# Routing weights on the down sums: router and experts of a fused attention and FFN kernel put into one block

## What is computed

```
x = x + ao @ wo
h = _rmsnorm(x, ln2_w)
logits = h @ router_w
probs = jax.nn.softmax(logits, axis=-1)
topv, topi = jax.lax.top_k(probs, TOPK)
topv = topv / jnp.sum(topv, axis=-1, keepdims=True)
weights = jnp.sum(jax.nn.one_hot(topi, E, dtype=h.dtype) * topv[..., None], axis=-2)
gate = jnp.einsum('bsd,edm->bsem', h, w_gate)
up = jnp.einsum('bsd,edm->bsem', h, w_up)
act = jax.nn.silu(gate) * up * weights[..., None]
moe = jnp.einsum('bsem,emd->bsd', act, w_down)
return x + moe
```

## Time and profile before

| | |
|---|---|
| median of three runs | 717.56 us |
| traced span of the profiled execution | 711.4 us |
| what lies around the span, by the median | 6.2 us |
| PE, DVE, ACT, POOL busy in the span | 602.2, 587.9, 454.6, 227.9 us |
| routing and logits, first logit matmul to the last weight | 548.5 to 556.4 us |
| weight columns spread by TensorE | 557.2 to 568.0 us |
| expert slabs, first gate matmul to last down matmul | 568.3 to 704.7 us |

### The profile page before, as it was taken

How to read it: one execution, slowest core, us unless ns; L and a number is a source line. 1 busy time by engine, 2 the same in 40 slices (tenths; PEclk the granted TensorE clock), 3 DMA queues, 4 the chain that set the end, 5 groups by cost and what they waited for, 6 DMA issues and landing times. The chain is left out here.

```text
span 711.4 us, 13311 instructions
## 1 busy us (share of the span) xinstructions
PE 602.2 (85%) x3580; PEld 492.3 (69%) x3580; DVE 587.9 (83%) x1282; ACT 454.6 (64%) x1094; POOL 227.9 (32%) x435
## 2 busy tenths in 40 slices
PE   2979889988999999899999336899997689797996
PEld 2757778767887778778787325666666577575885
DVE  4768899878898788998889747899983599979995
ACT  3657777766777677767777125888883356344563
POOL 1553334323333333333335354722132321414000
PEclk9989999999999999999999868999998699998999
DMA  8020000000000000000000002000000220200000
GB/s 255 17 54 2 2 29 3 1 1 0 0 30 0 1 0 0 0 0 1 1 1 1 1 4 82 1 1 0 0 0 1 78 77 2 77 1 0 0 0 29
DMA packets 15342, 13.48 MB, mean 19 GB/s; under 512 B 1984, under 2 KB 14656, under 8 KB 15296
## 3 DMA queue, kind: packets, MB, share of 16 engines
q1 hardware_dynamic: 15072, 12.94, 6.2%
q10 hardware_dynamic: 224, 0.03, 0.0%
HBM read 12.44 MB, written 0.52 MB: 18 GB/s over the span
## 5 line engine op out<-in xcount | busy, mean ns | idle before, releaser
L516 ACT ACTIVATE p_raw<-bank,bias 128x512 f32<-128x512 f32 x128 | 87.7, 688 | 43.1 <-DVE bias L587 39.4
L582 DVE TENSOR_REDUCE neg_max<-bank 128x1 f32<-128x512 f32 x128 | 86.9, 679 | 5.9 <-issue 4.0
L657 POOL TENSOR_SCALAR p_norm<-p_raw,rinv 128x512 f32<-128x512 f32 x128 | 87.0, 692 | 0.1
L606 DVE TENSOR_TENSOR pT_lo<-bank,pT_hi 128x512 fp32r<-128x512 f32 x128 | 82.4, 685 | 3.9 <-issue 2.3
L534 ACT ACTIVATE pT_hi<-bank 128x512 fp32r<-128x512 f32 x128 | 69.7, 599 | 24.9 <-PE bank L439 23.4
L1472 ACT ACTIVATE act_hi<-act_f 128x512 fp32r<-128x512 f32 x56 | 35.4, 632 | 58.9 <-DVE act_f L1515 58.8
L439 PE MATMUL bank<-ident,p_norm 128*128 128x128 f32 x512 | 66.8, 273 | 0.4 <-DVE pT_lo L606 0.4
L439 PEld LDWEIGHTS bank<-ident,p_norm 128*128 128x128 f32 x512 | 59.8, 141 | 9.3 <-issue 1.2
L451 PE MATMUL bank<-pT_hi,vals 128*128 128x256 f32 x256 | 64.9, 286 | 1.5 <-DVE o_lo L598 1.5
L451 PE MATMUL bank<-pT_lo,vals 128*128 128x256 f32 x256 | 64.0, 283 | 0.0
L426 PE MATMUL bank<-keys,q_hi 128*128 128x512 f32 x128 | 54.7, 427 | 3.0 <-ACT p_raw L516 2.8
(11 more groups left out here) (272 smaller groups left out, 1731.3 us busy)
## 6 DMA issues: line engine op xcount, KB each, us to landing
ctx_raw<-in_ctx SPq DMA_DIRECT2D x4, 512.0 KB, 4.7
wkv_raw<-in_L_xattn_Wkv SPq DMA_DIRECT2D x2, 1024.0 KB, 11.1
gu_raw<-in_L_ffn_w_gate SPq DMA_DIRECT2D x4, 448.0 KB, 3.6
gu_raw<-in_L_ffn_w_up SPq DMA_DIRECT2D x4, 448.0 KB, 4.3
dn_raw<-in_L_ffn_w_down SPq DMA_DIRECT2D x4, 448.0 KB, 5.1
wout_raw<-in_L_xattn_Wout SPq DMA_DIRECT2D x2, 512.0 KB, 14.8
x<-in_x SPq DMA_DIRECT2D x1, 512.0 KB, 6.8
wq_raw<-in_L_xattn_Wq SPq DMA_DIRECT2D x1, 512.0 KB, 10.2
```

The costliest lines, as they stand in the source:

```text
L516: act.activation(p_raw[:, h % 2, t, :], s_bank[t][:, :], ACT.Exp, bias=bias[:, h % H, t:t + 1], scale=X_SCALE, accum_out=row_sum[:, h % H, ...
L582: dve.tensor_reduce(neg_max[:, h % H, t:t + 1], s_bank[t][:, :], AX_X, ALU.max, negate=True).then_inc(max_s, 1)
L606: dve.tensor_tensor(pT_lo[:, h % 2, 2 * half:2 * half + 2, :], t_bank[half][:, :].rearrange("p (j n) -> p j n", j=2), f(pT_hi[:, h % 2, 2 ...
L657: pool.tensor_scalar(p_norm[:, h % 2, t, :], p_raw[:, h % 2, t, :], rinv[:, h % H, t:t + 1], 1.0, ALU.mult, ALU.mult).then_inc(p_norm_s, 1)
```

## The change

`route` and `experts` become one function, `route_and_experts`, with one block, and its loops are unrolled.

- The weights multiply the down sums. Slabs are taken in the order 0, 1, 2, 4, 5, 6, 3. The three slabs of one expert add up in their own bank `y_bank`; then VectorE's `weigh(i)` makes y_w = y_bank x wide, and GpSimd's `add(i)` adds it onto `acc` in SBUF. There are 16 such sums. Only the mixed slab, now the last of each seven, keeps up_w, and alone goes to `d_bank`.
- act_f of the other slabs is made from `u_bank` in PSUM and gate, in one operation. `u_bank` and `g_bank` are two deep instead of three.
- `wide` and `wide_mix` come by DMA: weights (128 tokens x 8) are transposed into 8 rows, copied to SBUF and to DRAM (`weight_rows`), and read back to all partitions by sixteen transfers on SP, two per expert. The fetches of the pairs 1 to 3 stand behind them on SP.
- The router's softmax and top two run on VectorE behind the first act_f; gate and up of the first slabs stand ahead of them on TensorE. h2T_lo is made by VectorE instead of GpSimd.
- The residual x1 + x2 is made by GpSimd (`x_sum`, behind the split of pair 1) and added by VectorE at the very end.

Its core; the routing arithmetic itself is unchanged:

```diff
+        g_bank, u_bank, y_bank, d_bank = ([bank(f"{n}_bank{i}") for i in range(2)] for n in "guyd")
...
+        SLAB = [*range(MIXED), *range(MIXED + 1, SLABS), MIXED]
+        U, UNITS_ALL = CH * SLABS, PAIRS * CH * SLABS
+        YS = PAIRS * CH * 2
...
         def _(sp):
-            with sp.Fori(1, PAIRS) as g:
+            sp.wait_ge(wT_s, CH)
+            sp.dma_start(rows, wT[:, :]).then_inc(rows_out, 16)
+            sp.wait_ge(rows_out, 16)
+            for g in range(PAIRS):
+                for i in range(2):
+                    e = 2 * g + i
+                    sp.dma_start(wide[:, e, :], rows[e, :].partition_broadcast(P)).then_inc(wide_in[g], 16)
+                    part = slice(0, SPLIT) if i == 0 else slice(SPLIT, P)
+                    sp.dma_start(wide_mix[part, g, :], rows[e, :].partition_broadcast(part.stop - part.start)).then_inc(wide_in[g], 16)
+            for g in range(1, PAIRS):
                 sp.wait_ge(k.split_s, g)
                 fetch_pair(sp, k, dram, g)
             for c in range(CH):
...
+                if n >= 2:
+                    pe.wait_ge(silu_s, n - 1)
+                    pe.wait_ge(mul_s, n - 1)
...
+            def down(n):
+                g, c, s = where(n)
+                pe.wait_ge(a_lo_s, n + 1)
+                i = expert_sum(n)
+                if i is None:
+                    to, first, done = d_bank[c], g == 0, g == PAIRS - 1
+                else:
+                    to, first, done = y_bank[i % 2], n % SLABS % MIXED == 0, n == last_slab(i)
+                    if first and i >= 2:
+                        pe.wait_ge(y_out_s, i - 1)
...
+            def weights_first():
+
+                pe.wait_ge(weights_s, 1)
+                for t in range(TT):
+                    last = pe.transpose(w_bank[t // 4][0:E, (t % 4) * P:(t % 4 + 1) * P], weights[:, t, :], k.ident[:, :])
+                    if t % 4 == 3:
+                        last.then_inc(wT_ps, 1)
...
+            for n in range(UNITS_ALL + 2):
+                if n < UNITS_ALL:
+                    gate_up(n)
+                if n == 2:
+                    weights_first()
+                if n >= 2:
+                    down(n - 2)
+                if n == UNITS_ALL - SLABS + 4:
+                    tokens_first(0)
...
+            def weights_first():
+
+                for c in range(CH):
+                    act.wait_ge(wT_ps, c + 1)
+                    act.activation(wT[:, c * BANK:(c + 1) * BANK], w_bank[c][0:E, :], ACT.Copy).then_inc(wT_s, 1)
...
+            for n in range(UNITS_ALL + 1):
+                if n >= 1:
+                    head(n - 1)
+                if n < UNITS_ALL:
+                    silu(n)
+                if n == 2:
+                    weights_first()
...
             split_pair(pool, k, 1, 1)
...
+            pool.tensor_tensor(x_sum[:, :, :], k.x1[:, :, :], x2[:, :, :], ALU.add).then_inc(x_sum_s, 1)
+
+            def add(i):
+
+                c = i // 2 % CH
+                pool.wait_ge(y_out_s, i + 1)
+                if i // 2 < CH and i % 2 == 0:
+                    pool.tensor_scalar(acc[:, c, :], y_w[:, i % 2, :], 1.0, 1.0, ALU.mult, ALU.mult).then_inc(added_s, 1)
+                else:
+                    pool.wait_ge(added_s, i)
+                    pool.tensor_tensor(acc[:, c, :], acc[:, c, :], y_w[:, i % 2, :], ALU.add).then_inc(added_s, 1)
+
+            for i in range(YS):
+                add(i)
+                if i % 4 == 3 and i // 4 + 2 < PAIRS:
+                    g = i // 4 + 2
+                    split_pair(pool, k, g, g % 2, (down_ps, (g - 1) * U))
...
+            def product(n):
+                g, c, s = where(n)
+                dve.wait_ge(gu_ps, n + 1)
+                if n >= 2:
+                    dve.wait_ge(a_lo_s, n - 1)
+                up = u_bank[n % 2][:, :]
+                if s == MIXED:
+                    dve.wait_ge(wide_in[g], 4 * 16)
+                    dve.tensor_tensor(up_w[:, :], up, wide_mix[:, g, c * BANK:(c + 1) * BANK], ALU.mult).then_inc(weighed_s, 1)
+                    dve.wait_ge(weighed_s, n // SLABS + 1)
+                    up = up_w[:, :]
+                dve.wait_ge(silu_s, n + 1)
+                dve.tensor_tensor(act_f[:, n % 2, :], up, gate[:, n % 2, :], ALU.mult).then_inc(mul_s, 1)
+
+            def tail(n):
+                dve.wait_ge(a_hi_s, n + 1)
+                dve.tensor_tensor(act_lo[:, n % 2, :], act_f[:, n % 2, :], f(act_hi[:, n % 2, :]), ALU.subtract).then_inc(a_lo_s, 1)
+
+            def weigh(i):
+
+                g, c, _ = where(last_slab(i))
+                dve.wait_ge(down_ps, last_slab(i) + 1)
+                dve.wait_ge(wide_in[g], 4 * 16)
+                if i >= 2:
+                    dve.wait_ge(added_s, i - 1)
+                dve.tensor_tensor(y_w[:, i % 2, :], y_bank[i % 2][:, :], wide[:, 2 * g + i % 2, c * BANK:(c + 1) * BANK], ALU.mult)\
+                    .then_inc(y_out_s, 1)
+
+            def summed(c):
+                dve.wait_ge(added_s, YS - (CH - 1 - c) * 2)
+                dve.wait_ge(down_ps, UNITS_ALL - (CH - 1 - c) * SLABS)
+                dve.tensor_tensor(sumT[:, c * BANK:(c + 1) * BANK], d_bank[c][:, :], acc[:, c, :], ALU.add).then_inc(sumT_s[c], 1)
+
+            def finished(c):
+                dve.wait_ge(out_ps, c + 1)
+                dve.wait_ge(x_sum_s, 1)
+                dve.tensor_tensor(res[:, 4 * c:4 * c + 4, :], by_tile(d_bank[c]), x_sum[:, 4 * c:4 * c + 4, :], ALU.add).then_inc(res_s[c], 1)
+
+            shifted_logits()
+            for n in range(UNITS_ALL + 3):
+                if 1 <= n <= UNITS_ALL:
+                    tail(n - 1)
+                if n < UNITS_ALL:
+                    product(n)
+                if n == 0:
+                    routing_weights()
+                if n >= 3 and (n - 3) % SLABS in (MIXED - 1, 2 * MIXED - 1):
+                    weigh(expert_sum(n - 3))
+                if n == UNITS_ALL - SLABS + 3:
+                    summed(0)
+                if n == UNITS_ALL - SLABS + 5:
+                    finished(0)
+            summed(1)
+            finished(1)
```

More of the change, by code:

```diff
@@ L1377, in _, with last_slab, half @@
+        def last_slab(i):
+            return i // 2 * SLABS + (i % 2 + 1) * MIXED - 1
+        def half(i):
+            return range(4 * i, 4 * i + 4)
         @block.sync
         def _(sp):
-            with sp.Fori(1, PAIRS) as g:
+            sp.wait_ge(wT_s, CH)
[8 more added lines that the diff above has]
+            for g in range(1, PAIRS):
@@ new lines, in _ @@
+            for i in range(2):
+                t = slice(4 * i, 4 * i + 4)
+                pool.wait_ge(sq_s, i + 1)
+                pool.tensor_scalar(mean_sq[:, t], sum_sq[:, t], 1.0 / D, RMS_EPS, ALU.mult, ALU.add).then_inc(mean_s, 1)
+                pool.wait_ge(mean_s, i + 1)
+                pool.tensor_tensor(rrms[:, t], mean_sq[:, t], k.inv_root[:, :].broadcast_to([P, TT // 2]), ALU.pow).then_inc(rrms_s, 1)
+            split_pair(pool, k, 1, 1)
+            pool.tensor_tensor(x_sum[:, :, :], k.x1[:, :, :], x2[:, :, :], ALU.add).then_inc(x_sum_s, 1)
@@ L1528, in _, with link @@
-            dve.wait_ge(sum_ps, 2)
-            dve.tensor_copy(sumT[:, BANK:TOK], d_bank[1][:, :]).then_inc(sumT_s[1], 1)
-            dve.wait_ge(out_ps, 2)
-            dve.tensor_copy(res[:, 4:8, :], g_bank[1][:, :].rearrange("p (t d) -> p t d", t=4)).then_inc(res_s[1], 1)
+            count = [0]
+            def link(ins):
+                count[0] += 1
+                ins.then_inc(step, 1)
+                dve.wait_ge(step, count[0])
+            for i in range(2):
+                dve.wait_ge(att_ps, i + 1)
+                dve.tensor_tensor(x2[:, 4 * i:4 * i + 4, :], k.z[:, 4 * i:4 * i + 4, :], by_tile(att_bank[i]), ALU.add).then_inc(x2_s, 1)
@@ new lines, in _ @@
+            for i in range(2):
+                dve.wait_ge(x2_s, i + 1)
+                dve.wait_ge(rrms_s, i + 1)
+                for t in half(i):
+                    last = dve.scalar_tensor_tensor(h2[:, t, :], x2[:, t, :], rrms[:, t:t + 1], k.ln2_row[:, :], ALU.mult, ALU.mult)
+                last.then_inc(h2_s, 1)
+            for i in range(2):
+                cols = slice(i * BANK, (i + 1) * BANK)
+                dve.wait_ge(hi_s, i + 1)
+                dve.tensor_tensor(h2T_lo[:, cols], h2T_bank[i][:, :], f(h2T_hi[:, cols]), ALU.subtract).then_inc(lo_s, 1)
@@ L1578, in build @@
         self_attention(nc, k, dram)
-        k.d_bank = [ctx.enter_context(nc.psum_tensor(f"d_bank{c}", [P, BANK], F32)) for c in range(CH)]
-        k.x2, k.weights = sb("x2", [P, TT, D]), sb("weights", [P, TT, E])
-        k.h2T_hi, k.h2T_lo = sb("h2T_hi", [P, TOK], F32R), sb("h2T_lo", [P, TOK], F32R)
-        route(nc, k, dram)
-        experts(nc, k, dram, out)
+        route_and_experts(nc, k, dram, out)
 def shape_constants():
```

400 lines of the change are left out of this document (136 added, 264 removed).

## The result

The changed kernel takes 736.3 us (median of four runs, 735.4 to 740.4) against 717.8 in the runs beside it: 1.028 times as long, 95% interval 1.0252 to 1.0308. The forecast was 724.4 us: the side was right, and the size, 6.8 us in place of 18.5, was not.

A forecast was written before the change was run, and what follows sets the result against it. Bound by TensorE (2.03 us a slab) and the act chain (1.99). Front gain 12.8, waits 3.4 and 18.5, then the loop: last act_f 709.3, plus end 8.9, span 718.2; with time around it 724.4 us, own range 717 to 731, overall 713 to 742.

The forecast's parts named there:

- the clean slab: Undisturbed slab of the expert loop: removing up_w shortens neither TensorE nor the act chain, so it stays at 2.0 us.
- the front: Start of the expert stage: second act_f at 561.9 instead of 574.68, a gain of 12.8 us, bounds 9 to 14.
- the order of the queue: SP queue: pair 1's fetch behind seventeen transfers lands at 593.9; a rival, chance 0.15, had it share engines, landing at 583.
- the chain behind it: After pair 1's fetch: split to 604.1, x_sum, first acc at 607.3; third y_w stalls 18.5 us, bounds 13 to 39.
- the end: After the last act_f, through last addition, transposes and output: 8.9 us, against 9.8 before.
- The spreads: Sixteen DMA transfers of weight rows: 1.3 us each, 20.7 for all; first y_w waits 3.4 us, bounds 0 to 8.
- The additions: GpSimd adding y_w onto acc: forecast no cost, starting second; rival, chance 0.22: they start first, 17 us more, 741.
- The splits and the clock: Loop after the stall: two splits hold act_lo 4.9 us each, 9.8 (6 to 14); TensorE's lowered clock costs 1.5 (0 to 4).
- Around the span: Time outside the traced span: 6.2 us, from the 711.4 us span and the timed median of 717.56, added at the end.

The follow-up runs named there:

- experiment 12: Changed kernel with the eight full-width spreads issued first, then the eight half-width ones, lower and upper in turn: 731.1 us, 1.0179.
- experiment 5: Changed kernel with pair 1's fetch behind pair 0's spreads and additions held until they meet no VectorE operation with two SBUF inputs: 711.7 us, 0.9928.
- experiment 3: Changed kernel with each GpSimd addition also waiting for the act_lo that follows the y_w: 731.7 us, 1.0247.
- experiment 6: experiment 5 with x_sum ahead of the split and each pair's full-width spreads ahead of its half-width ones, y_w waiting only for the former: 707.95 us, 0.9862.
- experiment 2: Changed kernel with the fetch of pair 1 issued after the four spreads of pair 0, ahead of the other twelve: 719.8 us, 1.0039.
- experiment 1: Changed kernel with the fetch of pair 1 issued before the weight rows are written and spread: 723.4 us, 1.0105.

## Why the prediction was right and where it failed

Right: the clean slab (1.99), the front (second act_f at 562.44 against 561.9), the order of the queue and the chain behind it (third y_w waiting for acc), and the end (9.2 us against 8.9). That the front came out within 0.6 us is in part luck, as the first act_f of this front scatters by 3.2 us over the runs.

In the traced span I was 15.0 us short (733.2 against 718.2). By the marks:
- **The spreads, a mis-sized term: 7.2 us.** The step that failed is "`wide[e]` (512 KB) costs 1.3 us and half a `wide_mix` (256 KB) 1.3, 2.6 per expert, 5.2 for the first pair, 20.7 for all". The two terms were nearly right where each kind runs alone (experiment 12: all sixteen in 21.9 us; full-width at 414 GB/s in the best stretch and 355 in the mean, halves at 236; the earlier trace rows had 336 for another full-width load, too), but they may not be added when the two kinds alternate: then it is 220 GB/s and 29.3 us. So the split came 8 us later, the third y_w 7.2 (614.47 against 607.3), and act_f of slab 13, at 616.93 against 609.8, carries it on.
- **The additions, a wrong step: some 12 us.** The step that failed is "0.06 of lateness gives act_lo the port; then the addition runs beside act_f and act_hi at no cost". They start first: 0.07 to 0.09 us after the end of y_w and 0.02 to 0.03 ahead of act_lo, in all nine cases away from splits and the end. I weighed 0.05 us of lead against 0.06 of semaphore waits and gave it 0.22. The second half of the sentence is right ahead of an unmixed slab (experiment 5) and wrong ahead of a mixed one (experiment 3: 1.35 us for 0.69). The trace of before has waits of GpSimd on VectorE to read this from, and the prediction uses none of them, for instance `d` behind `bias`, 64 times, where GpSimd starts 0.08 to 0.23 us after VectorE's end (median 0.18); these are tiny operations, and would have pointed further to the wrong side (one stands below the list). From slab 13 to the end there are 9 times 1.13 us, one of 0.7 before the end and two of 0.55 beside splits.
- **The splits and the clock, the other way: 4.8 us too dear.** The two stretches of seven slabs with a split take 19.87 and 19.37 us, 5.2 and 4.7 above the 14.7 of a clean one. 1.7 of it are additions, so a split costs 3.5 and 3.0 and not 4.9, what the clock took included, for which I had 1.5 more. 12.0 - 3.3 - 1.5 is 7.2 of the 7.6 us between act_f 13 and act_f 55 (107.1 against 99.5).
- **Around the span: 4 us, that hid part of it.** 6.2 - 2.2, from one quick trace set against a median. So the time is 11.9 us above the forecast where the span is 15.0.

The wait of GpSimd on VectorE in the trace of before, at one place:
```profile
103.54 0.16 DVE L587 SCALAR_TENSOR_TENSOR bias<-neg_max,s0n 128x1 f32<-128x1 f32 x1
...
103.88 0.20 POOL L647 TENSOR_TENSOR d<-bias,s0n 128x2 f32<-128x2 f32 x1 [1.09 <-DVE bias L587]
```

What the move of the weights from up rows to down sums is worth by itself no run shows, as all have the rest of the change too. The traces show two parts of it. In a clean stretch it costs: seven slabs took 14.28 us before and take 14.68 with the additions out of the way, since the up multiplications were free and the mixed slab costs 0.7 more. Beside a split it saves, since before also act_f, with both inputs in SBUF, was held (2.17 us for the one at 604.67), and with `u_bank` in PSUM it is not. From act_f 14 to act_f 55, with two splits in each, pass 100.5 us before, 105.1 in the changed kernel with its additions ahead of act_lo, and 97.5 in experiment 6. The first and last act_f of these stretches, but for the last of before, which is in the earlier trace rows, and the last of after, which is above at 724.00:
```profile
601.17 0.70 DVE L1515 TENSOR_TENSOR act_f<-up_w,gate 128x512 f32<-128x512 f32 x1
...
604.67 2.17 DVE L1515 TENSOR_TENSOR act_f<-up_w,gate 128x512 f32<-128x512 f32 x1
```
```profile
618.93 0.68 DVE L1505 TENSOR_TENSOR act_f<-u_bank,gate 128x512 f32<-128x512 f32 x1
```
```profile
600.18 0.68 DVE L1512 TENSOR_TENSOR act_f<-u_bank,gate 128x512 f32<-128x512 f32 x1
...
697.70 0.69 DVE L1512 TENSOR_TENSOR act_f<-up_w,gate 128x512 f32<-128x512 f32 x1
```
The gain at the front, 12 us at the second act_f and 14 at the first, is real; the one block, the weight rows by DMA and the gate and up matmuls ahead of the routing make it together, and no run separates them. The changed kernel lost it twice: once to the order of a queue (16.5 by experiment 2), once to 0.03 us on a shared port (8 by experiment 5, 12 by the marks).

## What to carry to other kernels

Before a transfer is moved, write down the queue that it will stand behind and who needs it next; here a few lines of order were worth 16 us. Ask also what an earlier landing sets free: it let a split run beside the router in experiment 1 and cost 8.4 us. Where GpSimd and VectorE both work from SBUF, ask of each pair which one starts first; if the one off the path wins, give it one more wait, and look at what it then lies beside. Don't add the time around a span from one trace and another run's median; read both from one execution.

## What the runs showed of the hardware

- A 128x512 addition on GpSimd that starts 0.03 us ahead holds a VectorE operation with both inputs in SBUF until it ends (0.69 to 1.82 us), one with an input in PSUM not at all (act_f from `u_bank` stays at 0.68 beside the additions of experiment 5); four small h2 operations went from 1.14 to 9.50 us beside a split. The Trainium skill (SBUF — State Buffer, "Who interferes with whom") has this exclusion, with the order of issue deciding; the traces agree for the case that GpSimd starts first.
- A DMA whose access starts with a dimension of 2 used two engines of sixteen, 53 GB/s, at the same bytes per row.
- Full-width spreads alone moved 355 GB/s in the mean and 414 in the best stretch, halves alone 236, both in turn 220; one DRAM row read 128 times (220 GB/s) is no slower than 128 rows (201).
- The transfers of one queue landed in the order of issue: a fetch behind all sixteen spreads let the split start at 602.02, the same one behind four of them at 582.65.
